# Layer 0's self attention: the causal mask by GpSimd's select on the product c instead of guard products, and the values' bias folded into the output bias

## The reference, cut to what matters

```python
g = x @ Wg.T + bg;  v = x @ Wv.T + bv          # 16 heads of 16
dot  = einsum('bhid,bhjd->bhij', g, g)
corr = dot / (|g_i| * |g_j| + 1e-8)
corr = corr * m                                 # m[i, j] = 1 for j <= i (causal), 0 after
corr = (corr + 1) / 2
denom = mean(corr, axis=3) + 0.5
fitness = 1 / (denom * sum(1 / denom, over i))
attn = softmax(corr * fitness * m + (1 - m) * NEG)
out  = (attn @ v) @ Wo.T + bo
x = layernorm(x + out)
```

## Time and profile before

| | |
|---|---|
| time, median of 3 runs | 2455.33 us (2452.11 to 2456.83) |
| the profiled execution's own time | 2453.8 us |
| its span, first to last instruction | 2452.1 us |
| mean granted TensorE clock | 0.971 |
| PE busy | 2262.6 us (92%) |
| PEld busy | 1768.8 us (72%) |
| DVE busy | 1347.3 us (55%) |
| ACT busy | 1100.5 us (45%) |
| POOL busy | 849.8 us (35%) |
| the pipeline over 32 tiles of this sublayer | from about 42.6 to 443.6 us of the span |

### The profile page before, as it was taken

The page is one execution under the profiler, slowest core; times in us unless marked ns, Lnnn a source line. Parts: engine busy times, 40 slices in busy tenths (PEclk is TensorE's granted clock), DMA queues, the critical chain, the costliest instruction groups (busy, mean ns, idle before and its releaser), DMA issues. The chain is left out here.

```text
span 2452.1 us, 44501 instructions
## 1 busy us (share of the span) xinstructions
PE 2262.6 (92%) x17122; PEld 1768.8 (72%) x17122; DVE 1347.3 (55%) x2517; ACT 1100.5 (45%) x1872; POOL 849.8 (35%) x873
## 2 busy tenths in 40 slices
PE   7999998799998899999999799999995999999993
PEld 5777776466666566757776688888884888888893
DVE  6888888488887680015545567888885111111113
ACT  3666666456565564543334255555552111111113
POOL 3555454244444582000101234455444122222221
PEclk8999999899999999999999899999997999999997
DMA  5435554100110679480211323333332856666665
GB/s 144 113 90 129 137 128 115 61 27 27 53 53 19 214 254 295 149 262 4 69 50 37 112 90 106 104 104 109 104 121 76 293 174 191 193 174 183 194 203 148
DMA packets 204609, 313.21 MB, mean 128 GB/s; under 512 B 63473, under 2 KB 183153, under 8 KB 191089
## 3 DMA queue, kind: packets, MB, share of 16 engines
q1 hardware_dynamic: 184336, 255.25, 33.6%
q0 software_dynamic: 13440, 17.90, 4.1%
q10 hardware_dynamic: 6624, 37.23, 3.9%
HBM read 188.88 MB, written 121.45 MB: 127 GB/s over the span
## 5 line engine op out<-in xcount | busy, mean ns | idle before, releaser
L2748 ACT ACTIVATE dec_area<-me_ps_h 128x512 f32<-128x512 f32 (+1 forms) x160 | 88.7, 554 | 423.8 <-PE me_ps_h L2726 423.8
L2789 DVE TENSOR_SCALAR me_yo<-me_ps_y,moe_xg 128x256 f32<-128x256 f32 x72 | 34.8, 484 | 429.2 <-PE me_ps_y L2736 391.3
L2664 POOL DMA_INDIRECT xo<-me_yo,me_row x72 | 112.7, 1565 | 410.7 <-DVE me_yo L2789 350.2
L2726 PE MATMUL me_ps_h<-me_xt,me_w 128*128 128x256 f32 (+1 forms) x1056 | 210.1, 357 | 0.0
L2736 PE MATMUL me_ps_y<-me_w,dec_area 128*128 128x256 f32 x944 | 209.2, 379 | 0.7 <-DVE me_yo L2789 0.7
L2199 POOL TENSOR_TENSOR l1x_e<-l1x_e,l1x_ri 128x1024 f32<-128x1024 f32 x64 | 121.7, 1901 | 240.8 <-DVE l1x_ri L2459 240.8
L2736 PEld LDWEIGHTS me_ps_y<-me_w,dec_area 128*128 128x128 f32 x944 | 179.0, 190 | 24.8 <-issue 1.1
L2726 PEld LDWEIGHTS me_ps_h<-me_xt,me_w 128*128 128x128 f32 x1056 | 181.9, 191 | 20.0
L882 POOL TENSOR_TENSOR l0x_e<-l0x_e,l0x_ri 128x1024 f32<-128x1024 f32 x64 | 120.0, 1896 | 186.9 <-DVE l0x_ri L1102 186.9
L2298 PE MATMUL l1x_ps_p<-l1x_xct,dec_area 128*128 128x256 f32 x512 | 126.4, 392 | 1.0 <-ACT l1x_xct L2384 1.0
L2336 PE MATMUL l1x_ps_o<-dec_area,l1x_ot 128*128 128x256 f32 x512 | 120.4, 389 | 1.4 <-ACT l1x_ot L2407 1.4
(11 more groups left out here) (414 smaller groups left out, 5335.5 us busy)
## 6 DMA issues: line engine op xcount, KB each, us to landing
me_w<-in_w SPq DMA_DIRECT2D x33, 2048.0 KB, 9.5
xs<-dec_zero SPq DMA_DIRECT2D x31, 1032.0 KB
k<-kv_kt ACTq DMA_DIRECT2D x16, 1024.0 KB, 5.5
v<-kv_va ACTq DMA_DIRECT2D x16, 1024.0 KB, 5.2
l1x_kt<-k SPq DMA_DIRECT2D x16, 1024.0 KB, 5.1
l1x_va<-v SPq DMA_DIRECT2D x16, 1024.0 KB, 5.8
moe_w_first<-in_w SPq DMA_DIRECT2D x7, 2048.0 KB, 9.8
moe_xg<-xs SPq DMA_DIRECT2D x32, 258.0 KB, 2.8
```

The source lines that it names most:

```text
L2664: pool.indirect_dma_start(token_rows, bass.IndirectOffsetOnAxis(row[:, j % 2, q:q + 1], 0), yo[:, j % 2, q, :], None, compute_op=ALU.add). ...
L2726: last = pe.matmul(ps_h[i % HB][:, f % 2, 0:P * size(j)], weights(j)[:, FFN * c + f * P:FFN * c + f * P + P], xt[:, j % 2, c, 0:P * size(j ...
L2748: act.activation(h[:, j % 2, 2 * i:2 * i + 2, 0:P * size(j)], ps_h[i % HB][:, :, 0:P * size(j)], ACT.Gelu).then_inc(gelued, 1)
```

## The change

The guard matrix goes (`after`, `guardb`, their memset, select and scaled copy), and with it the four guard products of each `score`; the eight products of L681 now start their PSUM part afresh. Above the diagonal c is now a number like any other, until GpSimd sets it to 0 in place by a new select `mask_c(n, u)`, of the same form as `mask_e`. `row_sums` and `weigh_odd` wait for it (semaphore `causal`). `mask_e` stays.

The values get no bias: ScalarE's `copy_v` takes the place of VectorE's `add_v`. Once, before the first tile's values, ScalarE spreads the bias column (`bvs`), TensorE multiplies it by the output weights (`multiply_bias`) and VectorE adds the product to the output bias (`fold_bias`). The order of GpSimd's list changes too.

```diff
 # l0_attn_project, GpSimd and ScalarE
-                act.wait_ge(after_cut, 1)
-                act.activation(guardb[:, :, :], after[:, :].unsqueeze(1).to_broadcast([P, 2, P]), ACT.Copy, scale=GUARD / -1e30).then_inc(guard_set, 1)
-                pool.memset(after[:, :], 0.0).then_inc(cleared, 1)
-                pool.wait_ge(cleared, 1)
-                pool.affine_select(out=after[:, :], in_=after[:, :], compare_op=ALU.is_ge, fill=-1e30, base=0,
-                                   pattern=[[-1, P]], channel_multiplier=1).then_inc(after_cut, 1)
 # l0_attn_heads, GpSimd
                 def weigh_odd(n):
                     item_done(pool, fit_done, n)
-                    item_done(pool, corr_done, 2 * n + 1)
+                    item_done(pool, causal, 2 * n + 1)
...
+                def mask_c(n, u):
+                    item_done(pool, corr_done, 2 * n + u)
+                    pool.affine_select(out=c[:, n % 2, u, :, :], in_=c[:, n % 2, u, :, :], compare_op=ALU.is_ge, fill=0.0, base=0,
+                                       pattern=[[0, HALF], [-1, P]], channel_multiplier=1).then_inc(causal, 1)
...
                 def bias_x(n):
                     if n == 0:
-                        pool.wait_ge(w_loaded, 64)
+                        pool.wait_ge(bo_done, 1)
...
-                walk([(2, bias_x), (3, last_of_group(roots)), (1, weigh_odd), (-2, pads), (1, lambda n: mask_e(n, 0)), (1, lambda n: mask_e(n, 1))])
+                walk([(1, weigh_odd), (-2, pads), (0, lambda n: mask_c(n, 1)), (1, lambda n: mask_e(n, 0)), (1, lambda n: mask_e(n, 1)),
+                      (2, bias_x), (3, last_of_group(roots)), (-1, lambda n: mask_c(n, 0))])
 # SP: the bias as a column of 128 x 2
-                sp.dma_start(b_v[:, :], bcast(bgv[D:2 * D])).then_inc(w_loaded, 16)
+                sp.dma_start(b_v[:, :], bvc).then_inc(w_loaded, 16)
 # VectorE
-                def add_v(n):
-                    if n == 0:
-                        dve.wait_ge(w_loaded, 64)
-                    item_done(dve, v_ready, n)
-                    slot_free(dve, applied, n, VR)
-                    dve.tensor_tensor(va[:, n % VR, :, 0:3:2, :], ps_a[1][:, 2:4, :]..., b_v[:, :]..., ALU.add).then_inc(v_biased, 1)
+                def fold_bias():
+                    dve.wait_ge(bv_multiplied, 1)
+                    dve.tensor_tensor(b_o[:, :], ps_e[1][:, 0:2, :].rearrange("p a b -> p (a b)"), b_o[:, :], ALU.add).then_inc(bo_done, 1)
...
                 def row_sums(n):
-                    item_done(dve, corr_done, 2 * n + 1)
+                    item_done(dve, causal, 2 * n + 1)
...
-                walk([(1, weigh_even), (0, add_v), (0, lambda n: correlate(n, 1)), (2, divide), (0, row_sums), (2, residual), (-1, lambda n: correlate(n, 0)), (0, fitness)])
+                walk([(1, weigh_even), (0, lambda n: fold_bias() if n == 0 else None), (0, lambda n: correlate(n, 1)), (2, divide), (0, row_sums), (2, residual), (-1, lambda n: correlate(n, 0)), (0, fitness)])
 # TensorE
+                def multiply_bias():
+                    pe.wait_ge(w_loaded, 64)
+                    pe.wait_ge(bv_spread, 1)
+                    for k in range(2):
+                        last = pe.matmul(ps_e[1][:, 0:2, :].rearrange("p a b -> p (a b)"), bvs[:, k, :], w_o[:, k, :], start=k == 0, stop=k == 1)
+                    last.then_inc(bv_multiplied, 1)
                 def project_v(n):
                     if n == 0:
-                        pe.wait_ge(w_loaded, 64)
+                        multiply_bias()
                     item_done(pe, ops_copied, n, 2)
-                    slot_free(pe, v_biased, n, 1)
+                    slot_free(pe, v_copied, n, 1)
...
-                    for q in range(4):
-                        pe.matmul(ps_s[:, q, :, 1, :], identb[:, :], guardb[:, :, :], start=True, stop=False)
                     for g in range(2):
                         for q in range(4):
                             last = pe.matmul(ps_s[:, q, g, 1, :], ops[32 * q:32 * q + 32, n % 2, u, g, :],
-                                             ops[32 * q:32 * q + 32, n % 2, u, 2 + g, :], start=False, stop=g == 1)
+                                             ops[32 * q:32 * q + 32, n % 2, u, 2 + g, :], start=True, stop=True)
 # ScalarE
+                act.wait_ge(w_loaded, 64)
+                act.activation(bvs[:, :, :], b_v[:, :].unsqueeze(2).to_broadcast([P, 2, P]), ACT.Copy).then_inc(bv_spread, 1)
+
+                def copy_v(n):
+                    if n == 0:
+                        act.wait_ge(va_zeroed, 1)
+                    item_done(act, v_ready, n)
+                    slot_free(act, applied, n, VR)
+                    act.activation(va[:, n % VR, :, 0:3:2, :], ps_a[1][:, 2:4, :]..., ACT.Copy).then_inc(v_copied, 1)
...
-                walk([(8, normalise), (2, lambda n: exponentials(n, 1)), (0, lambda n: guard(n, 0)), (2, copy_et), (0, lambda n: guard(n, 1)), (1, lambda n: exponentials(n, 0)), (-1, copy_ops)])
+                walk([(8, normalise), (2, lambda n: exponentials(n, 1)), (0, lambda n: guard(n, 0)), (2, copy_et), (0, copy_v), (0, lambda n: guard(n, 1)), (1, lambda n: exponentials(n, 0)), (-1, copy_ops)])
```

More of the change, by code:

```diff
@@ L186, in l0_attn @@
         norms = NormRoots(Kit(nc, stack, "l0n"), sq, n2, rn, lno, ln)
-        l0_attn_project(nc, xt_in, xt, wgv, bgv, ema, gamma, omega, gv, norms, ident, identb, after, guardb, lpad, rpad, kp)
-        l0_attn_heads(nc, x_in, xt, wgv, bgv, gv, norms, ident, identb, guardb, lpad, rpad, kp, wo, bo, toep, ah, x_out, xs, xo, zero, zeroed)
+        l0_attn_project(nc, xt_in, xt, wgv, bgv, ema, gamma, omega, gv, norms, ident, identb, lpad, rpad, kp)
+        l0_attn_heads(nc, x_in, xt, wgv, bgv, bvc, gv, norms, ident, lpad, rpad, kp, wo, bo, toep, ah, x_out, xs, xo, zero, zeroed)
         norms.kit.clear_semaphores()
@@ L236, in halve, with l0_attn_project @@
         dve.tensor_scalar(self.ln[:, at, :], self.ln[:, at, :], 0.5, None, ALU.mult).then_inc(self.halved, last - first)
-def l0_attn_project(nc, xt_in, xt, wgv, bgv, ema, gamma, omega, gv, norms, ident, identb, after, guardb, lpad, rpad, kp):
-    GUARD = -1e5
+def l0_attn_project(nc, xt_in, xt, wgv, bgv, ema, gamma, omega, gv, norms, ident, identb, lpad, rpad, kp):
     NP = TILES // 2
@@ L263, in l0_attn_project @@
         g_ready, g_biased = kit.sem("g_ready"), kit.sem("g_biased")
-        cleared, after_cut, one_set, identb_set, guard_set = (kit.sem(n) for n in ("cleared", "after_cut", "one_set", "identb_set", "guard_set"))
+        cleared, one_set, identb_set = (kit.sem(n) for n in ("cleared", "one_set", "identb_set"))
         names = ("coef_loaded", "sig_done", "pa_done", "q_done", "log_done", "coef_done", "age_set", "arg_done",
@@ L414, in l0_attn_heads @@
         w_v = kit.sb("w_v", [P, 2, D])
-        b_v = kit.sb("b_v", [P, D])
+        b_v, bvs = kit.sb("b_v", [P, 2]), kit.sb("bvs", [P, 2, P])
         va = kit.sb("va", [P, VR, HALF, 3, HD])
@@ L439, in l0_attn_heads @@
         ps_a = [kit.ps(f"ps_a{u}", [P, 4, P]) for u in range(2)]
-        names = ("w_loaded", "va_zeroed", "set", "blank", "parted", "v_ready", "v_biased", "l_padded", "r_padded", "transposed", "ops_copied",
-                 "scored", "tanh_done", "corr_done", "rows_summed", "denom_done", "inv_done", "inv_summed",
+        names = ("w_loaded", "va_zeroed", "set", "blank", "parted", "v_ready", "v_copied", "l_padded", "r_padded", "transposed", "ops_copied",
+                 "scored", "tanh_done", "corr_done", "causal", "bv_spread", "bv_multiplied", "bo_done", "rows_summed", "denom_done", "inv_done", "inv_summed",
                  "suminv_done", "fit_done", "weighted0", "weighted1", "exped", "masked", "e_transposed", "et_copied",
                  "applied", "inverted", "divided", "multiplied", "x_biased", "residual_done", "stats_done", "mv_done", "ln_step", "ln_done", "normed")
-        (w_loaded, va_zeroed, set_, blank, parted, v_ready, v_biased, l_padded, r_padded, transposed, ops_copied,
-         scored, tanh_done, corr_done, rows_summed, denom_done, inv_done, inv_summed,
+        (w_loaded, va_zeroed, set_, blank, parted, v_ready, v_copied, l_padded, r_padded, transposed, ops_copied,
+         scored, tanh_done, corr_done, causal, bv_spread, bv_multiplied, bo_done, rows_summed, denom_done, inv_done, inv_summed,
          suminv_done, fit_done, weighted0, weighted1, exped, masked, e_transposed, et_copied,
@@ L568, in _ @@
                 norms.halve(dve, LAST, norms.NC)
-                def add_v(n):
-                    if n == 0:
-                        dve.wait_ge(w_loaded, 64)
-                    item_done(dve, v_ready, n)
-                    slot_free(dve, applied, n, VR)
-                    dve.tensor_tensor(va[:, n % VR, :, 0:3:2, :], ps_a[1][:, 2:4, :].rearrange("p a b -> p (a b)").rearrange("p (j a d) -> p j a d", a=2, d=HD),
-                                      b_v[:, :].rearrange("p (j a d) -> p j a d", a=2, d=HD), ALU.add).then_inc(v_biased, 1)
```

(7 more changed lines are left out.)

14 lines of the change are left out of this document (7 added, 7 removed).

## The result

The changed kernel took 2436.8 us (median; 2435.87 to 2438.72), the kernel before 2454.5 beside it: a ratio of 0.9929 [0.9912, 0.9946]. Against the 2455.3 that the prediction started from, -18.5 us where -14.7 was forecast.

The account below looks back on a forecast made before the run. One closed loop of waits through TensorE, ScalarE and VectorE was taken to set the 11.48 us round. 29 x -0.54 = -15.7, +1 start, 0 tail: -14.7, so 2439.1 profiled, 2440.6 median; 8-in-10 range 2434 to 2449.

Parts of the forecast that it names:

- The loop: Correlation, residual sum, transposes with copy, scores and tanh form one loop of waits setting the round, 11.48 us.
- The guard products: TensorE's second-half score loses 0.54 us a round, bounds 0.40 to 0.61; 0.66 between L675 and L681 would confirm.
- The select on c: New GpSimd selects, 1.09 us each, hidden in both halves; second half has 0.88 to spare before the row sums.
- rival 2: GpSimd's select delays VectorE's row sums, by waiting for the reciprocal or taking 1.90: slower, about 2463 us; chance 0.06.
- The port rule: GpSimd and VectorE share an SBUF port lock; as written it adds no wait for the instructions beside the selects.
- 0.2 to spare: GpSimd's `bias_x` ends at +5.75, its residual on VectorE comes at +5.96: costs nothing, but the tightest place.
- The other 0.2: GpSimd is free after the pads at +12.0, the next second-half select is due at +12.23: costs nothing.
- Rival 1: The 0.2 distances on GpSimd aren't there, it takes over the loop, half the gain goes: 2448.5 us; chance 0.12.
- Values: VectorE loses a 0.42 us sum, ScalarE gains a 0.38 copy, both hidden; VectorE's idle time before the correlation 1.2.
- The start, +1: Pipeline start costs +1 us, ends -2.7 to +5.9; ScalarE's load wait +2.5, first two tiles' selects 1.2 each.
- rival 4: TensorE's added idle time could lower its clock; not expected in steady rounds, a cold start stretch within +5.9; no chance given.
- The sum: Whole kernel: 29 rounds at -0.54 give -15.7, start +1, tail 0, together -14.7 us.

Follow-up runs that it names:

- e2: Kernel before with only the values' bias folded into the output bias; guard products stay, no select on c: 2457.4 us, ratio 1.0004.
- e9: e7 with the residual's statistics also moved behind `weigh_even` of the next round: 2421.9 us, ratio 0.9865 to the kernel before.
- e5: Changed kernel with four useless wide bf16 products put ahead of both kinds of narrow ones in every score: 2451.0 us, ratio 0.999 to the kernel before.
- e6: Changed kernel with VectorE's residual sum moved ahead of the small scaling of the denominators: 2438.5 us, ratio 0.9944 to the kernel before.
- a0: The changed kernel run again without edits, as the measure for others: 2439.8 us, ratio 0.9941 to the kernel before.
- e8: Changed kernel with ScalarE's bias spreading and its wait for the loads moved behind the first operand copies: 2438.5 us, ratio 0.9936 to the kernel before.
- e10: e9 with the later bias spreading of e8: 2423.2 us, ratio 0.9871 to the kernel before.
- e3: Changed kernel with four useless wide bf16 products put between the two kinds of narrow ones in every score: 2458.7 us, ratio 1.001 to the kernel before.
- e4: Changed kernel with the second half's select on c done twice in a row: 2452.3 us, ratio 0.9978 to the kernel before.
- e7: e6 with GpSimd's `bias_x` also moved ahead of the second select on e: 2428.1 us, ratio 0.9887 to the kernel before.
- e1: Kernel before with the select on c replacing the guard products and GpSimd's new order; values' bias stays on VectorE: 2434.4 us, ratio 0.9897.
- e11: e1 with the residual sum and `bias_x` moved early as in e7: 2424.4 us, ratio 0.9885 to the kernel before.

## Why the prediction was right, and where its size was off

- **The loop** was right: correlation, row sums, residual, two quarters of transposes, score, tanh. What lies outside it left the round as it was, in the value sum (e2) and the statistics (e9) too.
- **The guard products are the term that was mis-sized.** "What it loses is the step from the start of L678 to the start of L681", 0.54, with an upper bound of 0.61: it was 0.75, outside the bounds. I took the blocks beside it as fixed and named 0.66 between them as a sign of being right; by starts each step is 0.11 shorter once they stand together, by ends it is the second block that takes 0.44 in place of 0.66 (e5), and I had bounded this effect on the side of a loss alone (0.40). Over 29 rounds the error is 29 x 0.21 = 6.1 us.
- **The select on c** costs what it was put down for, and hides where it was said to. Line L484, minimum/median/maximum in ns, then who waited for it (us, times), then one of those two places:

```profile
L484 POOL TENSOR_SCALAR_AFFINE_SELECT l0ah_c<-l0ah_c x64: 1093/1093/1099, 54.5 to 391.6; 128x1024 f32<-128x1024 f32 x64
```

```profile
  DVE l0ah_st L590: 2.4, 2
```

```profile
59.95 2.29 DVE L590 TENSOR_REDUCE l0ah_st<-l0ah_c 128x16 f32<-128x2048 f32 x1 [1.20 <-POOL l0ah_c L484]
```

  Those are the first two tiles, 1.2 each as in the upper end for the start. One select in each round lies beside the reciprocal (304.68 and 304.52 above) and is no longer for it: rival 2 fell. The port rule that I had weighed (the Trainium skill, "SBUF — State Buffer", on the engine side's ports) is written for two tensors read from SBUF; it foresees no wait here, and the rows agree: all 64 took 1093 to 1099 ns, one of each round beside the reciprocal.
- **"0.2 to spare" at the residual was 0.06 at most.** I compared the end of `bias_x` with the start of the residual and left out the hand-over, 0.13 to 0.23 where VectorE stands idle for it (e6). `bias_x` was just in time, and the forecast of "cost nothing" held with it. The other 0.2, from the pads to the next select, went with the shorter round: the pads end at 304.67 and the select starts at 304.68, at its +1.29. Rival 1 stood at its edge in both places.
- **Values**: the copy took 0.38 and is hidden. VectorE's idle time before the correlation is 0.93 where I expected 1.2; with the true size it would be 1.34 + 0.42 - 0.75 = 1.01.
- **The start, +1**: +0.37 from the clearing of `va` to the third tile in one execution, -0.65 in the other (a0: 39.77 against 40.42), and the clearing itself comes at 44.14 in one and 43.11 in the other. The term can't be told from zero, nor can the part of it that the load wait has, +2.5 on ScalarE in my working (e8, e10).
- **The clock** (rival 4): the granted clock of a steady round is 1.00 as before. From 60 to 90 us it is 0.89, and 0.94 in a0, where it was 0.97; that lies in the start.
- **The sum**: 29 x -0.75 = -21.8 in place of -15.7. Given back were 0.5 in stalls, 0.4 at the start, 0.8 in the tail, 1.4 before the heads (where the diff only takes work away) and 1.6 behind this sublayer (where it touches nothing). I had the last three at nothing. So the two errors partly cancel, and that the total is 3.8 off and not 6 is luck: -18.5 where -14.7 was forecast, near the fast end of the range.

## What to carry to other kernels

A block taken out of a chain gives back its own step and what it did to its neighbours: read the steps of the same neighbours where they stand together, and bound a term on both sides with them. A distance between an end on one engine and a start on another is spare only less the hand-over, so measure that where the waiter really waits. When a change has shortened a loop, follow the loop again: here the next 0.32 a round (10.73 to 10.41) was two instructions moved, one on each of the engines that meet at the residual; VectorE's alone gained nothing (e6).

## What the runs showed of the hardware

- Blocks of narrow products (16 or 32 rows, 16 recorded instructions each) start 0.55 apart behind each other and take 0.66 a step with wide products between them; four wide bf16 products of 256 columns cost 0.44 ahead of both and 0.75 between them (e3, e5). By ends, a step from 128-row to narrow products costs about 0.22 and one from narrow to wide about 0.11.
- A VectorE sum that waits for GpSimd's `bias_x` starts 0.23 after its end in most rounds of e6 and 0.13 to 0.14 in three, where other hand-overs in this loop are 0.04 to 0.07 (a select's end to the reduction in e4, 309.90 to 309.94; a correlation's end to a select, 304.61 to 304.68). In e4 the same pair is 0.09 apart (312.69 to 312.78), with small instructions of VectorE right before it; what sets the larger figure is open.
- TensorE stands still in a few places for 2 to 6 us with nothing recorded that it waits for. In the changed kernel this falls into the last round:

```profile
394.86 0.41 PE L719 MATMUL l0ah_ps_e<-l0ah_et,l0ah_on 128*32 128x128 f32 x3 [3.80 <-issue]
```

  As far as fourteen profiles tell, it follows the kernel and not chance. The last round is 14.41 here and 15.41 in a0, the same kernel, and 14.87 to 15.99 in e2, e4, e5, e6, e7 and e8, each time with such a stall at this product (3.80 to 5.70); it is 12.05 to 12.19 in the two kernels with the mask alone (e1, e11), with about 2 us at the product with the output weights; and it is 10.73 in the kernel before and e3 and 10.56 in e9 and e10, without one. So the changed kernel pays 3.7 us and more in its last round, which no forecast had. No edit was made for it, and what causes it no run tells; it is as large as the gain of many an edit: between e7 and e9 the last rounds differ by 4.3, the times by 6.2.
- Profiles and medians can differ by as much: e1 and a0 have equal rounds (10.73) and nearly equal spans (2437.0, 2436.6), yet their ratios are 0.0044 apart, since e1's profiled execution was its slowest.
